# Byte loads of an attention pass issued from ScalarE's queue instead of SyncE's

## The reference

```python
h = (x @ W).reshape(n, HEADS, HID)
e = leaky_relu(a_src[src] + a_dst[dst], 0.2)
m = segment_max(e, dst)
ex = exp(e - m[dst])
denom = segment_sum(ex, dst)
agg = segment_sum(h[src] * (ex / denom[dst])[:, :, None], dst)
out = relu(agg + bias) @ fc_w + fc_b
```

## Time and profile before

| what | value |
|---|---|
| time, median of 3 runs | 9093.38 us (9089.47 to 9102.39) |
| profiled execution, first to last instruction | 9046.9 us |
| PE, DVE, ACT, POOL busy | 63%, 64%, 25%, 71% of the span |
| mean granted TensorE clock | 0.733 |
| `attend_pairs`, first DMA issue to last message start | 3628.9 to 4199.3 us |

### The profile page before, as it was taken

How to read it: one execution, slowest core, us unless ns; L and a number is a source line. 1 busy time by engine, 2 the same in 40 slices (tenths; PEclk the granted TensorE clock), 3 DMA queues, 4 the chain that set the end, 5 groups by cost and what they waited for, 6 DMA issues and landing times. The chain is left out here.

```text
span 9046.9 us, 131904 instructions
## 1 busy us (share of the span) xinstructions
PE 5679.9 (63%) x35786; PEld 4627.8 (51%) x35874; DVE 5810.5 (64%) x15100; ACT 2292.8 (25%) x3456; POOL 6454.7 (71%) x5675
## 2 busy tenths in 40 slices
PE   0990024444488887698344442555559898989896
PEld 0440023333333333566333332555549898989896
DVE  9660035555577666556444446555559898989898
ACT  2000000000100000343222222222226565656564
POOL 4777767777377776674677772777758787878785
PEclk6995555555655555899666666887769999999998
DMA  1780035555599999895333342444457676767674
GB/s 40 289 308 2 2 84 131 131 131 131 101 213 211 210 210 183 263 290 168 88 82 81 80 73 67 128 129 128 130 118 221 191 221 189 219 190 222 190 221 142
DMA packets 1122974, 1403.89 MB, mean 155 GB/s; under 512 B 276858, under 2 KB 948302, under 8 KB 1109198
## 3 DMA queue, kind: packets, MB, share of 16 engines
q1 hardware_dynamic: 968942, 1098.82, 40.7%
q0 software_dynamic: 153312, 296.65, 17.0%
HBM read 1010.93 MB, written 383.96 MB: 154 GB/s over the span
## 5 line engine op out<-in xcount | busy, mean ns | idle before, releaser
L2437 PE MATMUL ps<-u,wide_r 128*128 x9280 | 1140.5, 277 | 129.3 <-issue 88.6
L2268 POOL TENSOR_TENSOR msg_r<-zo_r,share_r 128x1024 f32<-128x1024 f32 x580 | 1123.1, 1936 | 101.7 <-DVE share_r L2327 46.1
L2437 PEld LDWEIGHTS ps<-u,wide_r 128*128 128x128 f32 x9280 | 1092.2, 193 | 131.3 <-issue 131.2
L2449 PE MATMUL ps<-msg_r,hots_r 128*128 128x128 f32 x9280 | 1140.7, 276 | 24.4 <-POOL msg_r L2268 23.1
L2010 POOL DMA_INDIRECT z_r<-x_tab,src_row x880 | 854.4, 971 | 417.2 <-issue 268.0
L2449 PEld LDWEIGHTS ps<-msg_r,hots_r 128*128 128x128 f32 x9280 | 1081.8, 192 | 32.9 <-POOL msg_r L2268 31.9
L297 POOL DMA_INDIRECT rec_tab<-pay,row_i x831 | 808.0, 972 | 374.9 <-issue 275.1
L575 POOL DMA_INDIRECT ring<-y_tab,y_row x880 | 838.0, 952 | 306.9 <-issue 266.0
L1172 POOL DMA_INDIRECT ring_m<-t_tab,src_row x880 | 835.3, 949 | 307.9 <-issue 280.8
L1624 POOL DMA_INDIRECT ring_e<-t_tab,src_row x880 | 832.4, 946 | 271.7 <-issue 268.0
L2276 POOL TENSOR_TENSOR prod_r<-prod_r 128x512 f32<-128x512 f32 x580 | 735.0, 1267 | 319.2 <-DVE prod_r L2299 302.9
(11 more groups left out here) (303 smaller groups left out, 10622.4 us busy)
## 6 DMA issues: line engine op xcount, KB each, us to landing
zo_r<-zo_tab SPq DMA_DIRECT2D x2320, 192.0 KB, 2.8
ring_e<-k_tab SPq DMA_DIRECT2D x464, 260.0 KB
k_tab<-ring_m SPq DMA_DIRECT2D x220, 520.0 KB, 6.3
y_tab<-wide SPq DMA_DIRECT2D x100, 1024.0 KB, 3.9
zo_tab<-z_r SPq DMA_DIRECT2D x110, 512.0 KB, 3.6
hot_bytes_e<-hb_tab SPq DMA_DIRECT2D x464, 64.0 KB, 3.3
dl_b<-dl_tab SPq DMA_DIRECT2D x220, 128.0 KB, 3.8
zo_tab<-hot_bytes SPq DMA_DIRECT2D x220, 128.0 KB
```

The costliest lines, as they stand in the source:

```text
L2268: nc.gpsimd.tensor_tensor(msg[:, g % WR].rearrange("p c (k d) -> p c k d", d=CD), z_of(g).rearrange("p c (k d) -> p c k d", d=CD), share[: ...
L2437: last = nc.tensor.matmul(ps[:, 2 * (g % 2) + c // 4, c % 4 * D:(c % 4 + 1) * D], wide[:, g % WR, c, :], u[:, bass.ds(tiles[g % NO % 4 * O ...
L2449: last = nc.tensor.matmul(ps[:, 4 + g % 2, c // 2 * D:(c // 2 + 1) * D], hots[:, g % WR, c, :], msg[:, g % WR, c, :], start=c % 2 == 0, st ...
```

## The change

ACT issues the byte loads; SP keeps the rows, `acc` and its own register loads. ACT gets register loads of its own from the same table. Before its loop ACT issues the bytes of groups 0 to 3; from then on, at the end of loop k, it issues those of group k + 7. The rings, their sizes and all other streams stay as they are.

```diff
--- before.py
+++ after.py
@@ -1354,13 +1354,6 @@
                 with nc.Block() as block:
                     @block.sync
                     def _(sp):
-                        def bytes_in(g):
-                            if g >= HR:
-                                sp.wait_ge(s_hot, g - HR + 1)
-                            for a in range(OP):
-                                sp.dma_start(hb[:, g % HR, a], hb_tab[:, bass.ds(places[g // 4][g % 4 * OP + a], 2), :])\
-                                  .then_inc(s_hb[g % HR], 16)
-
                         def rows_in(g):
                             if g >= ZR:
                                 sp.wait_ge(s_msg, g - ZR + 1)
@@ -1369,18 +1362,14 @@
                                   .then_inc(s_row[g % ZR], 16)
 
                         places = {}
-                        for g in range(-HB_AHEAD, NO):
-                            if g + HB_AHEAD < NO:
-                                if (g + HB_AHEAD) % 4 == 0:
-                                    b = (g + HB_AHEAD) // 4
-                                    places.pop(b - 2, None)
-                                    places[b] = registers([mybir.EngineType.SP], pair_at, b * 4, NCH - 2)
-                                bytes_in(g + HB_AHEAD)
+                        for g in range(NO):
+                            if g % 4 == 0:
+                                places.pop(g // 4 - 2, None)
+                                places[g // 4] = registers([mybir.EngineType.SP], pair_at, g, NCH - 2)
                             if g == 2:
                                 sp.dma_start(acc[:, :, 0:W], t_tab[:, 0:W].rearrange("(t p) w -> p t w", p=P))\
                                   .then_inc(s_own, 16)
-                            if g >= 0:
-                                rows_in(g)
+                            rows_in(g)
 
                     @block.gpsimd
                     def _(pool):
@@ -1496,6 +1485,20 @@
                                 act.wait_ge(s_sum, (g - 1) * OP)
                             nc.scalar.activation(hots[:, g % WR], hot_bytes(g, P), ACT.Copy).then_inc(s_hot, 1)
 
+                        places = {}
+
+                        def bytes_in(g):
+                            if g % 4 == 0:
+                                places.pop(g // 4 - 2, None)
+                                places[g // 4] = registers([mybir.EngineType.Activation], pair_at, g, NCH - 2)
+                            if g >= HR:
+                                act.wait_ge(s_hot, g - HR + 1)
+                            for a in range(OP):
+                                act.dma_start(hb[:, g % HR, a], hb_tab[:, bass.ds(places[g // 4][g % 4 * OP + a], 2), :])\
+                                   .then_inc(s_hb[g % HR], 16)
+
+                        for g in range(HB_AHEAD + 2):
+                            bytes_in(g)
                         for k in range(-3, NO):
                             if 0 <= k + 1 < NO:
                                 exponential(k + 1)
@@ -1503,6 +1506,8 @@
                                 widen(k + 3)
                             if k >= 0:
                                 hot(k)
+                            if 0 <= k + 3 and HB_AHEAD + k + 5 < NO:
+                                bytes_in(HB_AHEAD + k + 5)
 
                     @block.tensor
                     def _(pe):
```

## The result

| | median | runs |
|---|---|---|
| before, beside it | 9094.90 us | 9089.47 to 9102.39 (4) |
| changed | 9016.12 us | 9012.46 to 9019.51 (4) |
| ratio | 0.9912 | 95% interval 0.9899 to 0.9925 |

The change makes the kernel 79 us faster. The forecast was 9014.

What follows compares the result with a forecast made beforehand. SyncE's unbroken DMA issue was taken to bound the first attention layer's second pass. 105 x (4.58 - 3.87) = 75 us, plus 5 at the start, made 80 off the timed 9093.4: 9014 us, range 9000 to 9072.

Steps and rivals of the forecast that it cites:

- Rival 4: Second pass, first attention layer: transfers, not their issue, make rows late, so nothing moves; 9093 us, chance 0.05.
- The floor: Second pass, first attention layer: TensorE's message matmuls allow no less than 3.795 us a group.
- The DMA engines: Second pass: almost full engines cost half of the groups some 0.15 us, so 3.87 us a group, gaining 75 us.
- Rival 1: Second pass: DMA engines bound it at 312 GB/s, 4.25 us a group; 35 us gained, 9058 us, chance 0.17.
- ScalarE's issues: Second pass, ScalarE's loop: the four added byte issues run beside its engine's work and cost nothing.
- rival 2: Second pass: ScalarE's issues don't overlap its engine's work; 4.38 us a group, 21 us gained, 9072 us, chance 0.10.
- Rival 3: Second pass: ScalarE's issues stand in line behind SyncE's; 5.7 us a group, 118 us longer, 9211 us, chance 0.06.
- The start: Start of the second pass: first rows and `acc` are issued earlier, gaining between nothing and 8 us, taken as 5.
- The lower end of the range: Whole kernel: 9000 us, from a floor of 3.795 us a group and the full 8 us at the stage's beginning.

Runs made afterwards that it cites:

- the second comparison: The changed kernel run again, unchanged, against the kernel before on another chip: 8952.00 us against 9042.92, ratio 0.9898.

## Why the prediction was right

**SyncE's issue was the bound.** Shown from three sides: fewer issues on the same queue give the whole gain (0.9902), four others put on it take most of it back (4.505 a group), and a longer lead without fewer issues gives nothing (1.0008). Rival 4, in which the transfers make the rows late whoever issues them, falls with the first.

**The floor is TensorE's.** 3.794 us a group, with TensorE at 388.00 of 388.00 us. The ends of matmuls are modelled in the profile, so the share alone wouldn't prove it; but TensorE waits for nothing in the list, while GpSimd, at 95%, waits for the exponential and the exponential for TensorE.

**The DMA engines lose nothing.** This term was mis-sized: I took 3.87 for groups lost to engines nearly full; it is 3.794, and 105 x (4.581 - 3.794) = 82.6 us instead of 75. The engines hold 352 GB/s for 388 us. Rival 1, a limit of 312, falls. How much above 352 they would go with a faster TensorE was not tried.

**ScalarE's issues cost nothing.** As taken: they run beside its engine, which excludes rival 2. Over 94 loops of the steady part the last of the four ends 1.6 us (median) before the next exponential. In five of them the exponential stood behind it, 0.10 us after its end; the pace didn't suffer.

**No line behind SyncE's issues.** Rival 3 had 0.84 us an issue on ScalarE. In the loop above four take 1.82 us, 0.49 from one start to the next with the register steps, no more than SyncE's 0.51. The start even shows a SyncE issue that stands still. Its timeline:

```profile
3679.82 4.32 SPq L1361 DMA_DIRECT2D ring_e<-k_tab  x8
3680.10 11.09 ACTq L1497 DMA_DIRECT2D hot_bytes_e<-hb_tab  x16
3684.19 0.68 SPq L1370 DMA_DIRECT2D acc<-t_tab  x1
3685.06 66.60 SPq L1361 DMA_DIRECT2D ring_e<-k_tab  x30
...
3692.46 1.82 ACTq L1497 DMA_DIRECT2D hot_bytes_e<-hb_tab  x4
...
3717.92 0.20 DVE L1404 TENSOR_TENSOR ps<-ps,ring_e 128x32 f32<-128x32 f32 x1 [19.27 <-DMA ring_e<-k_tab]
```

The lines of the two loads, issues in ns (min/median/max):

```profile
L1497 ACTq DMA_DIRECT2D hot_bytes_e<-hb_tab x464: 338/363/2239, 3680.1 to 4143.1; - x155
```

```profile
L1361 SPq DMA_DIRECT2D ring_e<-k_tab x464: 332/333/24021, 3679.8 to 4154.4; - x155
```

One row issue stands 24.0 us behind `acc`, from 3685.06 to 3709.08. In that time ScalarE issues four byte loads in 1.82 us, as in the steady loop. The first sixteen take 11.09 us, but there too the queues don't stand in line as a rule. The same timeline, in a narrower window:

```profile
3682.25 1.88 SPq L1361 DMA_DIRECT2D ring_e<-k_tab  x4
3682.49 1.98 ACTq L1497 DMA_DIRECT2D hot_bytes_e<-hb_tab  x4
```

Side by side, both queues issue four in about their usual time (1.89 and 1.82 us). The long ones of the sixteen are ScalarE's very first (2.24 us) and two right behind `acc` (1.11 and 0.61 us); what held these was not taken apart.

The Trainium skill, Perfetto Trace Analysis, section DMA Instruction — HWDGE (DVE, Sync), says that the descriptor generator is shared and that an issue waits for its lock. The 2.24 us of ScalarE's first issue could be such a wait. The four issues side by side show hardly any, and the 24.0 us in which ScalarE issued freely shows that an issue that stands still doesn't keep the other queue out.

**The start gave less.** This term was mis-sized too. The first rows are issued as SyncE's first work, as forecast. But the score that waits behind `acc` comes 3717.92 - 3679.82 = 38.1 us after the first row issue, against 40.4 from the first byte issue before: 2.3 us, where I took 5. The forecast let the data pass at 360 GB/s; the window of these 38.1 us, columns as in the earlier trace rows, shows 328:

```profile
3679.82:3717.92 38.10, 9.07 (x48) 7.03 (x48) 3.05 (x13) 5.34 (x7) 7.20 (x2) 0.54 1.04 328
```

Why the rate is lower was not tried. The first message comes 3.4 us later in the stage than before, behind ScalarE's first sixteen loads, and not where it was, as forecast; the score behind `acc` doesn't hang on it.

**The size was hit with some luck.** The sum is 82.6 + 2.3 = 85 us, the stage's 84.9, against the 80 of the prediction and the 79 of the timed runs (0.9912; in the second comparison 0.9898, or 91 us). So one term came out 7.6 us too small and the other 2.7 too large, and the 95% interval of the timed ratio runs from 68 to 92 us: that 80 and 79 lie so close is luck, the mechanism isn't. The pace of 3.794 lies just under the 3.80 to 3.97 that the forecast named. The lower end of the range is 9003 by its own terms, not 9000; nothing hangs on it.

**What was wrong and did no harm.** "The timed median is 9093.4, 46.5 more than the span, and I let that stand": nothing lies outside the span but 1.8 us. The profiled execution had a faster first pass. The forecast held because the sum of differences was put on the timed median; a forecast that had taken the span itself as the time (8967) would have been 49 us off.

The Trainium skill, DMA: Bandwidth & Descriptors, section Issuing engines are not separate DMA queues, says that issuing from more engines saves only the issuer's time, usually small beside the transfer. The first half agrees with these runs: one queue with fewer issues gains as much as two. "Usually small" doesn't: it was 4.36 of 4.58 us a group.

## What to carry to other kernels

Where a consumer waits for a DMA, look at the queue that issues it: without waits of its own and with issues of their usual length back to back, it is the bound, however busy the transfers look. (An issue that stands, like the one of 24.0 us behind `acc`, shows no wait either, and is no sign of this.) Count issues a period by their pitch (here 8 at about 0.5 us and 0.25 for register loads, 4.36 of 4.58 us) and take away enough of them, by a larger load or by another queue, to come under the next floor; beyond that nothing is gained. An engine whose waits are on the path can issue as long as its issues end before its next instruction is due: four cost the pace nothing, eight of a dearer form made the kernel 1.5% slower than before.

## What the runs showed of the hardware

- A load issued from ScalarE took 0.363 us of its queue with 128 partitions (64 KB) and 0.492 with 64 (32 KB): half the data, a longer issue. On SyncE a load of 16 partitions by 16 bytes took 0.420 (with four more loads), a load of rows 0.333 (changed kernel).
- The DMA share goes over 1: 1.04 at 352 GB/s for 388 us. A share of 0.93 in the kernel before was no limit.
- The same gathers of the first pass took about 50 us more or less from one profile to another, with waits of 1080.1 and 1131.1 us in it.
